# First attention moved into the second attention's buffers, batch 1's scores moved ahead of batch 0's experts, first rows split by VectorE, some loads issued later

## The reference

```python
x = x + _L0_xattn_ref(_layernorm(x), ctx, ctx, ...)      # 16 heads of 16, softmax
x = x + _L0_ffn_ref(_layernorm(x), gate_w, expert_w)     # 8 experts, the best one taken
x = x + _L1_xattn_ref(_layernorm(x), ctx, ...)           # 16 heads of 16, softmax under a fixed mask
x = x + _L1_ffn_ref(_layernorm(x), cn_w1, ...)           # three coupled cycles of a small network
x = x + _L2_xattn_ref(_layernorm(x), ctx, ctx, ...)      # linear attention with sigmoids
x = x + _L2_ffn_ref(_layernorm(x), W_lin, gate_w, left, right)   # linear map plus two of eight low-rank maps
x = x + _L3_xattn_ref(_layernorm(x), ctx, ctx, mask, ...)        # one head, softmax
x = x + _L3_ffn_ref(_layernorm(x), w_gate, w_up, w_down) # gated, integer weights, width 768
```

## Time and profile before

| | |
|---|---|
| median of 3 runs | 987.79 us (986.56 to 989.19) |
| span of the profiled execution | 986.1 us, 1.7 us under the median |
| PE busy | 949.3 us, 96% of the span, spins among it |
| spins (L2004) | 44.7 us, 336 products |
| DVE, ACT, POOL busy | 634.1, 536.3, 221.5 us |
| chain that ended last | 77% PE, 9% ACT, 8% DVE, 4% issue, 1% POOL, 1% DMA |
| HBM read, written | 41.67 MB, 13.89 MB |

### The profile page before, as it was taken

One profiled execution on the slowest core, in us unless ns is written; L12 is line 12 of the kernel. 1 busy time (PEld: TensorE's weight loads), 2 busy tenths in 40 slices (PEclk: granted clock), 3 DMA queues, 4 the chain that ended last, 5 costly groups with the idle time before them and its releaser, 6 DMA issues.

```text
span 986.1 us, 17493 instructions
## 1 busy us (share of the span) xinstructions
PE 949.3 (96%) x6126; PEld 702.7 (71%) x6126; DVE 634.1 (64%) x2245; ACT 536.3 (54%) x1097; POOL 221.5 (22%) x317
## 2 busy tenths in 40 slices
PE   8999999989999999999999999999999999999998
PEld 6665665757687766778687766776686757777777
DVE  4634674675675776867586776775776676736564
ACT  1341644776368643875448644866376544864421
POOL 3104311303240132403141023302321032012210
PEclk9999999999999999999999999999999999999999
DMA  7308535400540023520432104402132004000000
GB/s 261 58 30 226 127 113 113 88 10 17 113 94 9 11 50 70 113 49 13 80 73 46 44 1 86 98 11 49 27 67 59 12 17 92 1 12 1 1 1 22
DMA packets 41078, 58.27 MB, mean 59 GB/s; under 512 B 4096, under 2 KB 35840, under 8 KB 37376
## 3 DMA queue, kind: packets, MB, share of 16 engines
q1 hardware_dynamic: 39600, 48.59, 23.6%
q10 hardware_dynamic: 1392, 8.56, 2.3%
HBM read 41.67 MB, written 13.89 MB: 56 GB/s over the span
## 4 chain that ended last, share of the span: by engine, by line
PE 77%; ACT 9%; DVE 8%; issue 4%; POOL 1%; DMA 1%; ACTq 0%; SPq 0%; DVEq 0%; POOLq 0%
PE bank L1657 11%; PE bank L1984 6%; PE bank L1517 6%; PE bank L1736 6%; PE bank L1714 6%; PE bank L1508 6%; PE bank L1629 4%; PE bank L1995 4%; PE bank L1771 4%; PE bank L1765 3%; PE bank L1717 3%; ACT PT L886 2%; ACT QA L873 2%; PE bank L1797 2%; PE bank L1526 2%
## 5 line engine op out<-in xcount | busy, mean ns | idle before, releaser
L886 ACT ACTIVATE PT<-bank 128x512 f32<-128x512 f32 x256 | 153.0, 598 | 127.4 <-PE bank L1717 71.8
L1657 PE MATMUL bank<-w,xhT 128*128 128x512 f32 x256 | 126.8, 599 | 0.0
L1714 PE MATMUL bank<-QA,KA 104*128 104x256 bf16 x512 | 112.7, 273 | 12.4 <-ACT PT L886 10.5
L1184 DVE CUSTOM_DVE_ANT_0 bank<-bank,maskb 128x256 f32<-128x256 f32 x256 | 101.7, 450 | 25.7 <-PE bank L1629 25.4
L1177 DVE TENSOR_REDUCE mx<-bank 128x2 f32<-128x512 f32 x128 | 83.6, 684 | 28.9 <-PE bank L1629 28.5
L1629 PE MATMUL bank<-KA,QA 96*128 96x256 bf16 x512 | 91.1, 273 | 1.9 <-DVE mx L1184 0.8
L1984 PE MATMUL bank<-xhBT,wi 128*128 128x256 f32 x336 | 87.0, 390 | 2.9 <-DVE hT L1491 2.5
L1714 PEld LDWEIGHTS bank<-QA,KA 104*128 104x128 bf16 x512 | 46.5, 99 | 60.3 <-issue 45.8
L1230 DVE SCALAR_TENSOR_TENSOR x<-bank,one,x 128x256 f32<-128x256 f32 x128 | 61.5, 481 | 21.6 <-PE bank L1657 17.6
L873 ACT COPY QA<-bank 8x256 bf16<-8x256 bf16 (+1 forms) x128 | 67.8, 575 | 10.1 <-PE bank L1695 8.8
L1984 PEld LDWEIGHTS bank<-xhBT,wi 128*128 128x128 f32 x336 | 59.2, 191 | 12.9 <-DVE hT L1491 5.6
(11 more groups left out here) (311 smaller groups left out, 2028.3 us busy)
## 6 DMA issues: line engine op xcount, KB each, us to landing
QA<-scratch SPq DMA_DIRECT2D x90, 128.0 KB, 4.8
scratch<-kparts SPq DMA_DIRECT2D x30, 192.0 KB, 2.4
KA<-scratch SPq DMA_DIRECT2D x15, 384.0 KB, 4.6
scratch<-qparts SPq DMA_DIRECT2D x30, 192.0 KB, 2.3
KA<-scratch SPq DMA_DIRECT2D x15, 256.0 KB, 5.5
w<-pack ACTq DMA_DIRECT2D x1, 2345.0 KB, 8.3
wi<-ipack ACTq DMA_DIRECT2D x1, 2304.0 KB, 8.5
xin<-x_in SPq DMA_DIRECT2D x8, 256.0 KB, 6.3
```

The costliest lines, as they stand in the source:

```text
L886: act.activation(PT[:, n % RING, :, :].rearrange("p t s -> p (t s)"), st_bank[:, :], ACT.Exp).then_inc(exp_s, 1)
L1184: last = dve.tensor_tensor_reduce(s, s, maskb[:, t, :], op0=ALU.add, op1=ALU.max, scale=1.0, scalar=-HUGE, accum_out=mx[:, i % 4, n % GH, ...
L1657: last = pe.matmul(bank[n % 2][:, :], xhT[:, kk, t * P:(t + 1) * P], W("exp0", KT)[:, kk, i * 512:(i + 1) * 512], start=(kk == 0), stop=(k ...
L1714: last = pe.matmul(st_bank[:, t * S:(t + 1) * S], KA[m][0:KM, v, t * P:(t + 1) * P], QA[m][0:KM, v, :], start=True, stop=(m == 0))
```

## The change

Four things change. The first attention (0,0) lives in the buffers of m = 1 (HOME), and those of m = 0 are first used by batch 1; `before` says who used a buffer last. In `score`, heads(1,0) comes before experts(0) on PE and DVE. In the first rows, ACT writes the first parts of keys and queries straight from PSUM, DVE takes the copy of the transposed x from ACT and the key split from POOL (`cut`), and SP takes the copy of the first key part from ACT. Later come: the rows for the maxima of the other buffer, the values and the `third` of batch 0 (third(0) runs after the values of batch 1), and the loads of batch 1's context and x, the mask, batch 0's context, weight group 3 (which takes over what only `third` needs from group 2) and, on ACT, group 4. All five strings of TURNS are new; PE's has 2 w and 15 z instead of 106 and 54, and 18 spins instead of 8 stand ahead of the first wait. In the strings, PE's new order is seven p, four s, two p, two s, two v; ACT's begins with six p, the fifth and sixth being batch 1's keys, and then v; steps of heads(1,0) begin on PE after 20 steps of v.

```diff
--- before.py
+++ after.py
...
 EARLY, LATE = 280, 240
+SPINS = 18
...
-    ("wv0", P, KT * D), ("bv0", P, D), ("av", P, KT * D), ("bav", P, D), ("ao", P, KT * D),
-    ("diag", P, D), ("tri", P, H), ("pick", P, KT * H), ("ones", P, P),
+    ("wv0", P, KT * D), ("bv0", P, D),
     "cut",
     ("wo0", P, KT * D), ("bo0", P, D), ("gate0", P, KT * E), ("desc", P, E),
+    ("av", P, KT * D), ("bav", P, D), ("ao", P, KT * D),
+    ("diag", P, D), ("tri", P, H), ("pick", P, KT * H), ("ones", P, P),
     "cut",
...
     "tensor":
-        "pppwwwppwwwwwwwwwwwwwwwwppwwwwwwwwwwwwpwwwwwpwpwwwwwwppwwwwwwwwwwwwwwwwwwwsswwspspssvsvswwvsvpsvswwv"
...
+        "pppppppssssppssvvpssvsspvvspsvsvpsvvvpvpsvsvvvvvvvvpsvssvpsvsvpssvpssvpsvsssvsvssvvpvvpvsvpssvssvsss"
...
 PLACE = {bm: q for q, bm in enumerate(ATTENTIONS)}
+HOME = {(b, m): 1 if (b, m) == (0, 0) else m for b, m in ATTENTIONS}
...
+        def before(b, m):
+            users = [bm for bm in ATTENTIONS if HOME[bm] == HOME[b, m]]
+            return PLACE[users[users.index((b, m)) - 1]] + 1 if users[0] != (b, m) else 0
...
                 k_sent(sp, m, b)
-                if b:
-                    sp.wait_ge(st_ps, (PLACE[b - 1, m] + 1) * H)
+                if before(b, m):
+                    sp.wait_ge(st_ps, before(b, m) * H)
...
             def prepare(b):
                 if b == 0:
-                    sp.wait_ge(k_once[0], 16 * KT)
-                    again(KA[0], 0, 5, 1, k_first)
+                    sp.wait_ge(k_part, 1)
+                    for k in range(KT):
+                        sp.dma_start(KA[1][k * 8:(k + 1) * 8, :, :].rearrange("d h s -> d (h s)"), kparts[:, k, 0, :]
+                                     ).then_inc(k_once[0], 16)
                     sp.wait_ge(q_part, 1)
                     first_queries(0, 0, q_once[0])
                     yield
                     sp.wait_ge(q_part, 2)
                     first_queries(1, 3, q_once[1])
-                    sp.wait_ge(k_once[1], 16 * KT)
-                    again(KA[0], 0, 3, 2, k_first)
+                    sp.wait_ge(k_once[0], 16 * KT)
+                    again(KA[1], 0, 5, 1, k_first)
                     yield
                     sp.wait_ge(q_part, 3)
                     first_queries(2, 5, q_first)
+                    sp.wait_ge(k_once[1], 16 * KT)
+                    again(KA[1], 0, 3, 2, k_first)
...
+                    turned_ctx(1)
+                    sp.dma_start(xin[1][:, :, :], rows(x_in, 1)).then_inc(x_in_s[1], 16)
+                    load(3)
+                    yield
+                    sp.dma_start(att[:, :, :].rearrange("p t d -> p (t d)"), nomask).then_inc(nomask_in, 16)
+                    sp.dma_start(cin[:, :, :], rows(ctx_in, 0)).then_inc(c_in_s, 16)
...
             load(0)
             load(1)
-            sp.dma_start(cin[:, :, :], rows(ctx_in, 0)).then_inc(c_in_s, 16)
             load(2)
-            sp.dma_start(att[:, :, :].rearrange("p t d -> p (t d)"), nomask).then_inc(nomask_in, 16)
-            sp.dma_start(xin[1][:, :, :], rows(x_in, 1)).then_inc(x_in_s[1], 16)
-            load(3)
...
-                yield from split_k(b, 0)
-                if b == 0:
+                if b:
+                    yield from split_k(b, 0)
+                if b == 1:
+                    yield from split_q(b, 0, "p")
                     pool.wait_ge(w_in[3], 16)
...
+                if (b, m) == (0, 0):
+                    for dst, done in ((kparts[:, :, 0, :], k_part), (kf, k_f[0])):
+                        for k in range(KT):
+                            last = act.activation(dst[:, k, :], ps[:, k * S:(k + 1) * S], ACT.Identity,
+                                                  bias=W("bk0")[:, k:k + 1])
+                        last.then_inc(done, 1)
+                        yield
+                    return
...
+                if (b, m) == (0, 0):
+                    for k in range(KT):
+                        last = act.activation(qparts[0][:, k, 0, :], ps[:, k * S:(k + 1) * S], ACT.Identity,
+                                              bias=bqs[0][:, k:k + 1], scale=1.0 / HD ** 0.5)
+                    last.then_inc(q_part, 1)
...
             def prepare(b):
-                if b == 0:
-                    load(4)
-                    yield
+                yield from keys(b, 0)
...
                 yield from queries(b, 0, pb)
                 if b == 0:
+                    act.wait_ge(k_part, 2)
+                    first_keys(1)
                     act.wait_ge(k_split[0], 1)
-                    first_keys(1)
                     first_keys(2)
                     yield
+                    return
+                if b == 1:
+                    load(4)
+                    yield
+                    yield from third(0)
                 yield from third(b)
...
+            def cut(f, parts, part, done):
+                dve.tensor_tensor(parts[:, :, 1, :], f[:, :, :], parts[:, :, 0, :], ALU.subtract).then_inc(part, 1)
+                yield
+                link("p", dve.tensor_tensor(f[:, :, :], f[:, :, :], parts[:, :, 0, :], ALU.subtract))
+                dve.wait_ge(part, 2)
+                dve.tensor_tensor(parts[:, :, 2, :], f[:, :, :], parts[:, :, 1, :], ALU.subtract).then_inc(done, 1)
+                yield
+
             def first_split():
-                f, parts = qf[0], qparts[0]
+                dve.wait_ge(xh0T_ps, 1)
+                dve.tensor_copy(xh0T[:, :, :].rearrange("p k s -> p (k s)"), pb[:, :]).then_inc(xh0T_s, 1)
+                yield
+                dve.wait_ge(k_f[0], 1)
+                yield from cut(kf, kparts, k_part, k_split[0])
                 dve.wait_ge(q_f[0], 1)
...
+                yield from cut(qf[0], qparts[0], q_part, q_part)
...
             def score():
                 yield from heads(0, 0)
+                yield from heads(1, 0)
                 yield from experts(0)
                 for r in range(B):
-                    if r + 1 < B:
+                    if r and r + 1 < B:
                         yield from heads(r + 1, 0)
...
+                own_rows(1).then_inc(mask_ready, 1)
+                yield
                 own_rows(0).then_inc(mask_ready, 1)
-                yield
-                own_rows(1).then_inc(mask_ready, 1)
...
             def third(b):
-                pe.wait_ge(v_s[0], nth(v_s[0], b, 1))
+                pe.wait_ge(v_s[0], nth(v_s[0], max(b, 1), 1))
                 if b == 0:
-                    pe.wait_ge(q_f[0], 1)
+                    pe.wait_ge(w_in[3], 16)
+                elif b == 1:
+                    pe.wait_ge(third_act, 3)
...
                 elif b:
-                    pe.wait_ge(third_act, nth(third_act, b - 1, 3))
+                    pe.wait_ge(q_f[0], 1)
...
+                if b == 0:
+                    return
+                if b == 1:
+                    yield from third(0)
                 yield from third(b)
...
-                        last = pe.matmul(s_bank[n % 2][:, t * S:(t + 1) * S], QA[m][0:KR, u, t * P:(t + 1) * P],
-                                         KA[m][0:KR, u, :], start=True, stop=True)
+                        last = pe.matmul(s_bank[n % 2][:, t * S:(t + 1) * S], QA[home][0:KR, u, t * P:(t + 1) * P],
+                                         KA[home][0:KR, u, :], start=True, stop=True)
...
-                pe.wait_ge(max_s, (PLACE[b - 1, 1] + 1) * H if b else H)
+                pe.wait_ge(max_s, (PLACE[b - 1, 1] + 1 if b else PLACE[1, 0] + 1) * H)
...
-            for _ in range(8):
+            for _ in range(SPINS):
                 spin(la)
```

## The result

The changed kernel takes 1009.95 us (median of 4 runs, 1008.35 to 1013.1) against 987.63 for the kernel before: ratio 1.0235, 95% interval 1.0211 to 1.0259. It is slower by 22 us, and the forecast of 980.4 with its range to 990 was wrong. The profiled execution has a span of 1011.3 us, 25.2 more than before; it is the longest of the four, 3.1 us above the median, so about 3 of the 25.2 us are its own.

A forecast was written before the change was run, and what follows sets the result against it. PE time was taken as the bound, busy 949.3 of 986.1 us. Gains of 2.6 and 5.8 us, less 1.0 for the clock, gave 978.7 us span, 980.4 with 1.7 to the median; own range 974.5 to 984.8, outer 968 to 990.

The forecast's parts named there:

- First score: First rows: SBUF copies of 1.54 MB at 126 GB/s put it at 25.5 us (22.4 to 27.5) instead of 35.32.
- First attention: Batch 0's first attention: first transposed score at 33.0 us, output product at 64.5, experts' transposes at 71.2, 2.6 us earlier.
- third(0) has only moved from the first hole to the second: Five context-sum steps of batch 0, moved behind batch 1's projections: taken to cost PE nothing.
- The second hole: PE's spare time from 35.2 to 73.8 us, in the first attention: 12.9 us, taken as room for work.
- These 5.8 us come off in full: After the experts' transposes: 16 heads of (1,0), 4.8 us, and five value(1) steps, about 1, already done.
- The first rival: Ahead of heads(1,0): batch 1's queries land at 60, PE waits 9.6 us, 6 us lost, 986.4 us; chance 0.17.
- heads(0,1) do not become the wait: Second attention: its queries come some 29 us before needed; about 25 us of other PE work fills the wait.
- I see no part of it in the body: The packed stretch behind the first stages: none of the 8.4 us gain was placed there.
- The clock: Last batch after 890 us, 39 of 54 spins gone: 1 us charged for one half-rate stretch, bounds 0 and 14.
- the second rival: Last batch at half rate for most of its products: 14 us lost, 993.4 us; chance 0.09.
- the 14.8 us wait: SP's first wait, for ACT's key copy, ahead of the SBUF copies in the first rows: claimed to go.
- the forecast 8.4: Whole gain in us: 2.6 by the experts' transposes and 5.8 for work done ahead, before the clock charge.

The follow-up runs named there:

- e14: After with the loads SP issues from 25 us on held until the first queries' copies have landed; one run, first score at 31.7 us.
- e7: After with e2's spin products, e4's earlier load of the last layer's weights and e5's later order together; 993.2 us (1.0059).
- e8: e7 with third(0) and its loads put back ahead of the first score, where before has them; 1000.4 us.
- e10: After with before's order of scores and experts from the first attention on, added spins, and third(0) put back ahead of the first score; 1004.8 us.
- e13: e11 with batch 1's context for the third layer loaded where before does, and 36 spin pairs ahead of the first score; 985.6 us (0.9972).
- e2: After with 124 more pairs of spin products, 66 of them ahead of the first scores; 1005.9 us (1.0187).
- e4: After with the load of the last layer's weights issued at about 90 us instead of 121.3; 1004.5 us (1.0193).
- e5: After up to about 220 us, with before's order on all five engines from there on; 1003.4 us (1.0169).
- e12: e11 with batch 1's scores ahead of batch 0's experts, behind the twentieth value step, and e7's order after that; 1000.5 us (1.0129).
- e15: e13 with batch 1's scores ahead of batch 0's experts, behind the whole first attention, and e7's order after that; 1001.5 us (1.0138).
- e11: e10 with before's order on all engines from the first score on and 42 spin pairs ahead of it; 993.4 us (1.0058).
- e3: Before with its 106 pairs of early spin products taken out; 995.5 us (1.0076).

## Why the prediction was wrong, step by step

**First score: 32.0, forecast 25.5 with an upper bound of 27.5.** The rate was mis-sized. I took 126 GB/s from a window in which loads from memory ran too; copies alone make 95 (e14), and 1.54 MB at that rate are 16 us instead of 12.2. They do not run at it from the start either: the first key copies are issued at 9.87, as forecast, but the query copies follow at 13.2, and from 12 to 16 us 62 GB/s move (e14). The repeats are copies of copies: 3.9 us of SP's 5.59 us at 19.45 are a wait for the first ones to land. The note that copies bound by their own rate give 27.5 "or later" had the mechanism and too small a price. Cost: 6.5 us against the forecast.

**First attention: 48.6 us from first score to output product, forecast 39.0.** The first transposed score came 8.0 us behind the first score, near the forecast 7.5; from there to the output product it took 40.6 us instead of 31.5. The step that failed is "third(0) has only moved from the first hole to the second". The second hole was no hole: there product and exponential alternate, and what is put between two of them on PE or ACT lengthens the chain. At the full clock, from first transposed score to output product, third(0) costs 3.0 us (e7 to e8), the swapped scores 1.6 (e10), the way projections and copies are woven in 4.2 (e13); that leads from 36.8 us, in e2 and e7, to 27.9, in e13 and before. The rest up to 40.6 is the lower clock and its scatter (37.7 in e4 and e5). Spare time of PE in a window was read as room; it was PE's share of somebody else's period.

**"These 5.8 us come off in full": 3.0 came off at the full clock (e12), 0.8 at the clock that e15 had, and ahead of that the swap costs more than it gives.** On an unstretched attention it puts the network's first turn 13 us later (e15 against e13) or 7 us (e12 against e11, whose own wait of 3.74 us it does not have). The prediction had DVE's 0.684 us for each maximum, but let 14 of 16 hide in the 10.5 us in front of the output product. For that the queries had to land at 54, 28.5 us behind the first score; on an unstretched attention the scores could begin 35.4 us behind it (e12). The parts were written out 21.4 us behind the first score instead of 18.5, and the way through memory took 14 us instead of 10. Then the maxima stand on the chain in front of the experts. In after the stretch hides this: there the queries are landed when batch 1's scores begin, at 66.6. The first rival (the wait moves to batch 1's queries) was thus right on the transfer, 34.5 us behind the first score and a wait of 9.6, measured 10.4 in e12; its price, 6 us, was too low.

**"heads(0,1) do not become the wait":** they did, by the load on ACT's queue that met the write to memory (9.65 us instead of 2.3). That load is not in the diff; its time relative to the rest was moved. It cost 5.4 us by the medians, 3.7 by the stretch (e4).

**"I see no part of it in the body":** 7.9 us of the span (e5, median 6.6). The prediction put this term at nothing without a reason, though all five strings were new. That the later order costs this is shown; which of its steps do is open.

**The clock.** I charged 1 us, in the last batch. The last batch lost nothing (94.61 us, clock 0.98), as said; the second rival is refuted at its place. Its mechanism came in the first 200 us: PE stands from 14 to 32 us, the granted clock falls to 0.50 (1.2 of 2.4 GHz) by 20 us, and returns in parts only; window of after:

```profile
20.00:24.00 4.00, 0.00 (x0) 0.00 (x0) 1.45 (x3) 0.00 (x0) 0.00 (x0) 0.50 0.95 92
```

Its price is 4.0 us (e2), 8 in before's order (e3). The Trainium skill ("TensorE: Matmul & The Clock Gate", section "Part 1: The HAM clock gate") says that activity releases the throttle; the trace agrees, and it was I who set its place aside.

**Right:** the key projection, DVE's splits, the end of the 14.8 us wait, nothing lost with the late spins. Without its reordering the change does gain, 2.8 us (e13) of the forecast 8.4, but not where it was forecast: at the experts' transposes 0.1 us is left of the earlier first score.

The cures that were tried add up so: 1010 less clock 4.0, collision 5.4 and later order 6.6 gives e7's 993 to 994. The remaining 6 us to before can be read from e7's stretches: its first score is 2.8 us earlier, the first attention 11.9 longer, the way on to the experts' transposes 2.0 longer, and from there to the network's first turn it is 4.6 shorter, which leaves it 6.4 us late there. Within the first attention these are third(0), the weaving, the swap and the lower clock at its start; the totals of these on one common base were not measured.

## What to carry to other kernels

Spare time of an engine inside a stage where two engines take turns is not room: count whose period it is, and price a step put there at its full length until a run shows otherwise. Compare two stretches at the same granted clock: of the 4.6 us between e7 and e8 1.5 were the slow start and not the step taken out. When steps are reordered, list what each later transfer will newly meet, and compare the order of every engine to the end and not only where the change is meant. Work done ahead pays only if the next chain does not have to wait for it: here a shared bank made the experts wait for the maxima of the work done ahead.

## What the runs showed of the hardware

Copies inside SBUF, each into 8 to 32 partitions here, moved 93 to 96 GB/s with the DMA engines up to 97% busy (e14). The weight loads of after moved far more at the same share; window of after from 95 to 100 us:

```profile
95.00:100.00 5.00, 5.00 (x15) 2.35 (x13) 2.59 (x6) 0.00 (x0) 0.00 (x0) 1.00 0.98 420
```

The Trainium skill ("DMA: Bandwidth & Descriptors", section "Why small descriptors are slow (HBM only)") says that transfers from SBUF to SBUF do not suffer from small descriptors; no run here shows whether that holds, only that these copies ran at less than a quarter of the loads' rate. What makes them slow (rows, partitions, queue) was not tried.
